# The down product of the routed slots, from one fp32 product to three fp32r passes

## What is computed

```python
logits = x @ router_w.T
top_vals, top_idx = jax.lax.top_k(logits, 1)          # one of 8 experts for each token
scores = sigmoid(logits where chosen, -inf elsewhere)
gate, up = split((x * score) @ gate_up_proj[e])        # 256 -> 2 x 512
routed = (up * silu(gate)) @ down_proj[e]              # 512 -> 256
shared = silu(x @ shared_gate_w) * (x @ shared_up_w) @ shared_down_w
out = layernorm(x + shared + routed)
```

## Time and profile before

| | us |
|---|---|
| median of 3 runs | 579.01 (578.83 to 580.04) |
| the profiled execution | 578.61 |
| its span in the profile | 576.8 |
| PE busy | 558.0 (97%) |
| DVE busy | 391.8 (68%) |
| POOL busy | 302.8 (52%) |
| ACT busy | 225.6 (39%) |

### The profile page before, as it was taken

How to read it: one execution, slowest core, us unless ns; L and a number is a source line. 1 busy time by engine, 2 the same in 40 slices (tenths; PEclk the granted TensorE clock), 3 DMA queues, 4 the chain that set the end, 5 groups by cost and what they waited for, 6 DMA issues and landing times.

```text
span 576.8 us, 11184 instructions
## 1 busy us (share of the span) xinstructions
PE 558.0 (97%) x3732; PEld 458.9 (80%) x3732; DVE 391.8 (68%) x826; ACT 225.6 (39%) x403; POOL 302.8 (52%) x311
## 2 busy tenths in 40 slices
PE   7998989999999999999999899999999999999994
PEld 5776778788788788788787687888888888888883
DVE  5888987878877877877876786555644544445543
ACT  3434532553552552552542674133333333333331
POOL 0544592492492492492482555347675555555544
PEclk9999999999999999999999999999999999999998
DMA  7901207203203204501281503822343222222211
GB/s 259 299 6 38 74 2 52 97 1 75 74 1 75 74 2 74 183 2 38 76 362 40 219 19 98 269 57 67 72 84 85 83 74 82 68 80 82 75 47 36
DMA packets 37430, 50.48 MB, mean 88 GB/s; under 512 B 10576, under 2 KB 29520, under 8 KB 37360
## 3 DMA queue, kind: packets, MB, share of 16 engines
q1 hardware_dynamic: 28128, 31.24, 19.0%
q0 software_dynamic: 6048, 15.39, 9.5%
q10 hardware_dynamic: 3200, 3.15, 1.6%
HBM read 36.21 MB, written 13.96 MB: 87 GB/s over the span
## 4 chain that ended last, share of the span: by engine, by line
PE 84%; DVE 5%; issue 4%; POOL 3%; ACT 1%; DMA 0%; POOLq 0%; DVEq 0%; ACTq 0%
PE duo L1484 47%; PE duo L1856 11%; PE duo L1706 6%; PE duo L1540 5%; PE duo L1562 4%; PE duo L1866 3%; PE duo L1696 1%; PE duo L1750 1%; PE duo L1710 1%; PE duo L1644 1%; POOL turned L819 1%; PE duo L1686 1%; PE duo L1602 1%; PE duo L1620 1%; DVE sims L1009 1%
## 5 line engine op out<-in xcount | busy, mean ns | idle before, releaser
L1484 PE MATMUL duo<-w_gu_hi,xsT 128*128 x312 | 107.0, 404 | 0.0
L1484 PE MATMUL duo<-x1T,wsgu 128*128 128x512 f32 x384 | 93.1, 395 | 0.0
L1484 PEld LDWEIGHTS duo<-x1T,wsgu 128*128 128x128 f32 x384 | 70.9, 188 | 15.3
L1433 DVE SCALAR_TENSOR_TENSOR eh<-duo,seat,e_act 128x512 f32<-128x512 f32 x39 | 29.3, 751 | 76.9 <-PE duo L1484 72.0
L1856 PE MATMUL duo<-w_dn,ehT 128*128 x312 | 73.9, 380 | 0.8 <-ACT ehT L802 0.8
L819 POOL TENSOR_TENSOR turned<-turned,swapped 128x1024 f32<-128x1024 f32 x16 | 38.5, 2425 | 67.2 <-DVE swapped L1000 67.2
L938 POOL DMA_INDIRECT out_rows<-of,seat x39 | 39.7, 1018 | 55.8 <-DVE of L1452 52.8
L1484 PEld LDWEIGHTS duo<-w_gu_hi,xsT 128*128 128x128 f32 x312 | 58.6, 188 | 11.3
L1856 PEld LDWEIGHTS duo<-w_dn,ehT 128*128 128x128 f32 x312 | 56.3, 190 | 7.1 <-issue 1.0
L1484 PE MATMUL duo<-w_gu,xsT 128*128 x156 | 60.6, 389 | 0.0
L1009 DVE TENSOR_TENSOR sims<-duo,causal 128x512 f32<-128x512 f32 x64 | 41.2, 686 | 15.9 <-ACT sims L594 15.9
(11 more groups left out here) (171 smaller groups left out, 1131.8 us busy)
## 6 DMA issues: line engine op xcount, KB each, us to landing
w_gu<-L_ffn_gate_up_proj SPq DMA_DIRECT2D x8, 1024.0 KB, 8.3
x_in<-x_t SPq DMA_DIRECT2D x8, 512.0 KB, 6.4
x_res<-L_attn_x SPq DMA_DIRECT2D x8, 512.0 KB, 4.0
xz_d<-zs SPq DMA_DIRECT2D x8, 512.0 KB
xz_d<-x SPq DMA_DIRECT2D x7, 512.0 KB, 4.9
w_dn<-L_ffn_down_proj SPq DMA_DIRECT2D x4, 512.0 KB, 6.2
w_dn<-L_ffn_down_proj ACTq DMA_DIRECT2D x4, 512.0 KB, 8.2
rot<-rotation SPq DMA_DIRECT2D x4, 256.0 KB, 6.9
```

Of the source, the lines that this page charges most:

```text
L1433: nc.vector.scalar_tensor_tensor(out=eh[:, :], in0=duo[s % 2][:, 1, :], scalar=f32(seat[:, s, :])[:, 2:3], in1=e_act[:, :], op0=ALU.mult, ...
L1484: last = mm(out_, left(a, k), right(b, k), start=start and k == 0 and n == 0, stop=stop and k == kt - 1 and n == len(PASSES) - 1)
```

## The change

The down product of the slots is made in three fp32r passes. The high halves of the down weights (`w_dn`, now fp32r) stay on chip for all experts. The low halves don't fit there beside them. In steps 2 to 6 (one expert in steps 2 and 3, two in 4 to 6) the raw weights of one expert are loaded (SP), rounded to `dn_top` (ACT), subtracted to `dn_low` (POOL), and both halves written to DRAM (SP). `w_dn` is then filled from the high halves in DRAM, for experts 5 to 7 at the end of step 7 where it was in step 6. In the slots SP loads the low half of the slot's expert, 512 KB, into a ring of three. The low half of `ehT` is made by DVE from PSUM. `ehT_lo` lies over `wo`, the ring `dn_rest` over `x1T` and `x1`, and `dn_raw`, `dn_top`, `dn_low` where w_dn of experts 5 to 7 comes to lie.

```diff
+RESTS = 3
+PARTED = {2: (0,), 3: (1,), 4: (2, 3), 5: (4, 5), 6: (6, 7)}
...
+        dn_hi_d = scratch("dn_hi_d", [EXPERTS * P, FT * D])
+        dn_lo_d = scratch("dn_lo_d", [EXPERTS * P, FT * D])
...
+        dn_rest = sb("dn_rest", [P, RESTS, FT * D], F32R)
...
# SP, in step(t)
+                if t - 1 in PARTED:
+                    down_parts_out(PARTED[t - 1][-1])
+                if t in PARTED:
+                    down_raw_in(PARTED[t][0])
                 if has(t - 2):
                     sp.wait_ge(sig.x1_ok, TILES * (t - 1))
...
-                if t == PAIRS - 2:
-                    down_in(5)
-                    down_in(6)
-                    down_in(7)
...
+                if t in PARTED and len(PARTED[t]) > 1:
+                    down_parts_out(PARTED[t][0])
+                    down_raw_in(PARTED[t][1])
                 if has(t - 2) and t < PAIRS:
                     sums_out(t - 2)
+                if t == PAIRS - 1:
+
+                    sp.wait_ge(sig.dn_top_out, 16 * EXPERTS)
+                    sp.wait_ge(sig.dn_low_out, 16 * EXPERTS)
+                    down_in(5)
+                    down_in(6)
+                    down_in(7)
...
+            def down_raw_in(e):
+
+                sp.wait_ge(sig.dn_low_ok, e)
+                sp.dma_start(dn_raw[:, :].rearrange("p (k n) -> p k n", k=FT), down[e].rearrange("(k p) n -> p k n", p=P))\
+                    .then_inc(sig.dn_raw_in, 16)
+
+            def down_parts_out(e):
+                rows = slice(P * e, P * (e + 1))
+                sp.wait_ge(sig.dn_low_ok, e + 1)
+                sp.dma_start(dn_hi_d[rows, :], f32(dn_top[:, :])).then_inc(sig.dn_top_out, 16)
+                sp.dma_start(dn_lo_d[rows, :], f32(dn_low[:, :])).then_inc(sig.dn_low_out, 16)
...
+            def rest_in(s):
+
+                if s >= RESTS:
+                    sp.wait_ge(sig.ed_ps, s - RESTS + 1)
+                e = sp.value_load(slot_ei[0:1, one(s)], min_val=0, max_val=EXPERTS - 1)
+                sp.dma_start(f32(dn_rest[:, (s + 2) % RESTS, :]), dn_lo_d[bass.ds(e * P, P), :])\
+                    .then_inc(sig.rest_in[s % RESTS], 16)
...
# SP, before and in the slots
-            for s in range(5):
+            for s in range(3):
                 seat_load(s)
 
+            sp.wait_ge(sig.zs_ok, 2 * (PAIRS - 1))
+            sp.wait_ge(sig.x1_out, 16 * PAIRS)
+            rest_in(0)
+            for s in range(3, 5):
+                seat_load(s)
+
+            sp.wait_ge(sig.gu_ps, 2 * FT * PAIRS)
+            rest_in(1)
             sums_out(PAIRS - 1)
+            rest_in(2)
...
+            for s in range(RESTS, SLOTS):
+                rest_in(s)
+                if ahead < EARLY:
+                    for _ in range(3):
...
# ACT
+            def down_top(e):
+
+                act.wait_ge(sig.dn_raw_in, 16 * (e + 1))
+                if e:
+                    act.wait_ge(sig.dn_top_out, 16 * e)
+                    act.wait_ge(sig.dn_low_ok, e)
+                nc.scalar.activation(dn_top[:, :], dn_raw[:, :], ACT.Copy).then_inc(sig.dn_top_ok, 1)
...
                     shared_act(f, 0)
                     h_high(f, 0)
+                    if t in PARTED:
+                        down_top(PARTED[t][0])
                     shared_act(f, 1)
...
                     if t == 3:
                         expert_hi(EXPERTS - 2)
+                    if t in PARTED and len(PARTED[t]) > 1:
+                        down_top(PARTED[t][1])
...
             for e in range(4):
-                act.dma_start(w_dn[:, e, :, :], down[e].rearrange("(k p) n -> p k n", p=P)).then_inc(sig.edn_in, 16)
+                act.dma_start(f32(w_dn[:, e, :, :]).rearrange("p f d -> p (f d)"), dn_hi_d[P * e:P * (e + 1), :])\
+                    .then_inc(sig.edn_in, 16)
...
# POOL
+            def down_rest(e):
+
+                pool.wait_ge(sig.dn_top_ok, e + 1)
+                if e:
+                    pool.wait_ge(sig.dn_low_out, 16 * e)
+                nc.gpsimd.tensor_tensor(dn_low[:, :], dn_raw[:, :], f32(dn_top[:, :]), ALU.subtract)\
+                    .then_inc(sig.dn_low_ok, 1)
...
                     residual(a)
+                if t in PARTED:
+                    down_rest(PARTED[t][0])
                 if has(f) and t <= PAIRS:
                     take_seats(f)
+                if t in PARTED and len(PARTED[t]) > 1:
+                    down_rest(PARTED[t][1])
...
# DVE
+            def hidden_lo(s):
+
+                dve.wait_ge(sig.ehT_ok, s + 1)
+                if s:
+                    dve.wait_ge(sig.ed_ps, s)
+                nc.vector.tensor_tensor(ehT_lo[:, :, :], duo[2][:, 0, :].rearrange("p (f n) -> p f n", f=FT),
+                                        f32(ehT[:, :, :]), ALU.subtract).then_inc(sig.ehT_low_ok, 1)
...
                     slot_sum(s - 1)
+                if is_slot(s):
+                    hidden_lo(s)
...
# PE
             def slot_down(s, e):
-                pe.wait_ge(sig.ehT_ok, s + 1)
+                pe.wait_ge(sig.ehT_low_ok, s + 1)
+                pe.wait_ge(sig.rest_in[s % RESTS], 16 * (s // RESTS + 1))
...
                 for f in range(FT):
-                    last = mm(duo[2][:, 1, 0:D], ehT[:, f, :], dn_flat[:, bass.ds(e * (FT * D) + f * D, D)],
-                              start=(f == 0), stop=(f == FT - 1))
+                    weights = (dn_flat[:, bass.ds(e * (FT * D) + f * D, D)],
+                               dn_rest[:, (s + 2) % RESTS, f * D:(f + 1) * D])
+                    for n, (left, right) in enumerate(PASSES):
+                        last = mm(duo[2][:, 1, 0:D], halves[left][:, f, :], weights[right],
+                                  start=f + n == 0, stop=f == FT - 1 and n == len(PASSES) - 1)
```

More of the change, by code:

```diff
@@ L172, in build @@
         sb = tensors(ctx)
[L173 removed]
+        w_dn = sb("w_dn", [P, EXPERTS, FT, D], F32R)
         w_gu = sb("w_gu", [P, EXPERTS, KT, 2 * FF])
@@ L192, in build @@
         eh = sb("eh", [P, FF])
-        ehT = sb("ehT", [P, FT, P])
+        ehT = sb("ehT", [P, FT, P], F32R)
         of = sb("of", [P, OUTS, D])
@@ L357, in build @@
             edn_in = new("edn_in")
+            dn_raw_in = new("dn_raw_in")
+            dn_top_ok = new("dn_top_ok")
+            dn_low_ok = new("dn_low_ok")
+            dn_top_out = new("dn_top_out")
+            dn_low_out = new("dn_low_out")
+            rest_in = [new(f"rest_in{i}") for i in range(RESTS)]
+            ehT_low_ok = new("ehT_low_ok")
             ew_hi = new("ew_hi")
@@ L540, in _ @@
             sp.wait_ge(sig.scat, 16 * (NTILE - TILES))
-            for s in range(5):
+            for s in range(3):
                 seat_load(s)
+            sp.wait_ge(sig.zs_ok, 2 * (PAIRS - 1))
[5 more added lines that the diff above has]
+            rest_in(1)
             sums_out(PAIRS - 1)
-            for s in range(5, EARLY):
+            rest_in(2)
+            for s in range(5, 11):
                 seat_load(s)
-            sp.wait_ge(sig.plan_ok, 4)
-            sp.wait_ge(sig.scat, 16 * NTILE)
-            for s in range(EARLY, SLOTS):
-                seat_load(s)
+            ahead = 11
+            for s in range(RESTS, SLOTS):
+                rest_in(s)
+                if ahead < EARLY:
+                    for _ in range(3):
+                        if ahead < EARLY:
+                            seat_load(ahead)
+                            ahead += 1
+                elif s >= 13 and ahead < SLOTS:
+                    if ahead == EARLY:
+                        sp.wait_ge(sig.plan_ok, 4)
+                        sp.wait_ge(sig.scat, 16 * NTILE)
+                    for _ in range(2):
+                        if ahead < SLOTS:
+                            seat_load(ahead)
+                            ahead += 1
             sp.wait_ge(sig.out_done, 16 * SLOTS)
@@ L1835, in _ @@
                        w_gu[:, :, :, :].rearrange("p e k n -> p (e k n)").bitcast(F32R))
+            halves = (ehT, ehT_lo)
             dn_flat = w_dn[:, :, :, :].rearrange("p e f n -> p (e f n)")
```

20 lines of the change are left out of this document (13 added, 7 removed).

## The result

The changed kernel takes **572.21 us**, median of 4 runs (570.0 to 572.99), beside 578.92 of the kernel before on the same chip (4 runs, 578.58 to 580.04). The ratio is 0.9873, 95% interval 0.985 to 0.9896. The forecast was 570.3 us, 567.8 to 575.0: the sign is right, the median lies in the stated range, and 1.9 us of the gain did not come. The profiled execution took 572.99 us, the slowest of the four, 2.1 of it around its span.

A forecast was written before the change was run, and what follows sets the result against it. PE was taken as the bound, busy throughout slots and attention steps. Terms -10.6 + 0.65 + 0.9 + 0.4 = -8.65 took the profiled 578.61 to 569.96, stated as 570.3 us; range 567.8 to 575.0, own range 567.8 to 572.

The forecast's parts named there:

- The slots' down product: PE in the slots: twelve fp32r passes at 0.1215 us replace 1.73 us, saving 0.272 per slot, 10.6 us over 39.
- Rival C: Slots' down product: PE's sequencer sets the pace or register-addressed passes are no faster; 579 to 581 us, chance 0.05.
- Rival D: Nothing is blocked and passes take 0.120 us: 567.9 us, lower end of the forecast's range, sharing its 0.70 chance.
- "Cost 0" for the new DVE step in the slots: `hidden_lo`, 0.68 us per slot, fits DVE's idle time with 1.4 us left, so it costs nothing.
- the 0.3 feared for `eh` in four slots: Routing plan behind `hidden_lo` on DVE in slots 2, 4, 6, 7: at most 0.3 us each if cover were gone.
- The sentence on bandwidth: Slots: 73 GB/s now, 108 more from the fetch; gathers on the same DMA engines are issued slots ahead of use.
- rival B: Low half lands late in the slots, PE waits at `rest_in`; at 15 us delay 594 us, chance 0.06.
- The fetch itself: SP's 512 KB load per slot lands within 9.3 of the 13.1 us available, so it costs nothing.
- Step 2: POOL's `down_rest` subtraction blocks DVE's small `spot` and `hT_lo`, lengthening PE's wait at `shared_down`: +0.9 us.
- Steps 3 to 6: Making low halves: +0.4 us (0 to 0.9) in step 3, where a shift has no slack; 0 in steps 4 to 6.
- rival A: Steps pay more: ACT waits for second raw loads in steps 4 to 6, DVE against POOL; 572 to 575.7 us, chance 0.19.
- The tail: Last slot: nothing covers `hidden_lo` and its handover before the down product, +0.65 us.

The follow-up runs named there:

- e1: Changed kernel with no low-half fetch from slot 3 on, stale ring contents used instead: 569.36 us, ratio 0.9837.
- e4: Changed kernel with DVE's `slot_norm` placed behind `slot_sum` and `hidden_lo` in each slot: 572.27 us, ratio 0.9878.
- e8: e3 with `slot_norm` behind `slot_sum` and `hidden_lo`, the old order kept in the last rounds: 568.45 us, ratio 0.9827.
- e9: e8 with DVE's second `hT_lo` in step 2 made between the two halves of the group norm: 566.45 us, ratio 0.979.
- e11: The changed kernel, unchanged, run again in the session of the other experiments: 570.7 us, ratio 0.9862.
- e10: The kernel before with only the second `hT_lo` in step 2 moved between the group norm's halves: 576.58 us, ratio 0.9962.
- e2: Changed kernel with the low halves of steps 2 and 3 both made in step 3: 568.94 us, ratio 0.9841.
- e3: Changed kernel with POOL's low-half subtraction in step 2 moved behind the seat scatters: 568.78 us, ratio 0.9827.
- e5: e3 fetching only 64 of 128 partitions of each low half from slot 3 on: 570.02 us, ratio 0.9844.
- e6: e3 with the whole low half fetched in rows of 1 KB instead of 4 KB: 569.76 us, ratio 0.9839.
- e7: The kernel before with one extra DVE addition ahead of the `hT_lo` PE waits for in step 2: 579.94 us, ratio 1.0016.

## Why the prediction was right, and where it was wrong

**The slots' down product** (-10.6): right, and a little small. The period fell by 0.295 instead of 0.272, since the passes go at 0.120 us; that is 11.2 for the 38 intervals between 39 slots, where the forecast's figure is 10.3, and the slots of e1, e4, e8 and e9 show 11.0 to 11.3 (195.65 against 184.36 to 184.63). Rival C is refuted by the same rows; the small matmuls at 0.059 were the right evidence against it. Rival D's pace came, but not its clear path.

**"Cost 0" for the new DVE step in the slots**: this step failed. It held `hidden_lo` against DVE's own load, 1.4 us left, and that was right: the 0.3 feared for `eh` in four slots did not come. What it did not ask is what stands ahead of `hidden_lo` on DVE and waits for another engine. `slot_norm` does, for POOL, which waits for a landing, and the change adds the traffic that makes the landing late. It cost 2.7 us in the profiled execution and 0.5 in others. The sentence on bandwidth looked at the fetch and the gathers only; the scatters were named in rival B, but as a load on the fetch. For the gathers it counted on their being issued early enough; single ones were late for PE after all, by 0.2 to 0.5 us.

**The fetch itself**: right. It landed in 4.4 us, where 12.0 were left after its issue (13.1 - 1.1), so rival B is refuted. Its suspicion of the shared DMA engines was sound, only the transfer that suffered was the other one.

**Step 2** (+0.9): the block between POOL and DVE was right. The small operation was blocked too, by 0.57 us, as taken. PE's wait grew by this 0.57, not by 0.9: the subtraction ended at 84.24, which is 83.98 in the times of the trace before, 0.2 sooner than taken, and `spot` ended with it, where the 0.9 had let it begin there. By the Trainium skill (SBUF — State Buffer, Who interferes with whom) the lock holds for the whole instruction; the trace agrees, `spot` takes 0.76 us instead of 0.19, ending with POOL's 2.81. What was missing is the clock: in most runs of the changed kernel, and in e11, it costs another 1.5 us, more than twice the 0.57. The price of a PE wait was taken as its length.

**Steps 3 to 6** (+0.4): nothing at all. The outputs of steps 2 to 7 follow each other at 43.1 us, as before. ACT did wait for the second raw load in each of steps 4 to 6 (1.06, 1.09 and 2.58 us), the place that rival A named, but its copy in step 4 ended at 178.84, 4.1 us ahead of its next work, and PE has no wait from it. Rival A is refuted, though its time range fits the result: 572 came from two other places.

**The tail** (+0.65): right. +0.35 was measured from the last hidden transposes to the end, and this stretch holds the last of the 39 shorter down products, so the forecast's own figure for it is 0.65 - 0.27 = +0.38. The step from the hidden transposes to the last down product grew by 0.72 (2.10 against 1.38), where 0.75 was forecast.

The sum by what was measured in the profiled execution: -11.3 in the slots as e1 shows them undisturbed, +2.7 of slot waits, +0.57 and +1.5 in step 2, +0.35 at the end, +0.26 start-up, is -5.9. The forecast's own terms measure -11.3 + 0.57 + 0 + 0.35 = -10.4, where it had -8.65; e8, in which the two unforeseen costs are all but absent (0.2 us in the slots, a fallen clock in one run of five), stands at 568.45 against 578.69, -10.2. The two, the slots' waits and the clock, are 4.2 in this execution. That the median missed the forecast by 1.9 only is in part luck: the forecast's own terms came out 1.7 us better than it had them, against the 4.2. And 572.21 lies just above the forecast's own range, which ended at 572; the stated range holds it because it was widened to 575.0 for rival A, which did not happen.

**What stays open**: what decides whether the clock falls behind a given wait, and why the scatters' lateness reaches PE by 0.5 us in one execution and 2.7 in another, and whether the last pair's seat scatters on POOL have a part in it.

## What to carry to other kernels

When a new step is put into an engine's queue, its cover isn't the idle time of that engine alone: look at what stands ahead of it and waits for someone else, and follow that wait to its end, to a DMA's landing if it goes there. A large prefetch that is itself never late can still hurt, through the small transfers whose completions somebody waits for one by one. And a wait of some 2 us on a TensorE that is otherwise always busy should be priced at more than its length, and closing it by a change of order (here worth 2.2 us to the kernel before, e10) comes before any arithmetic.

## What the runs showed of the hardware that was not expected

- The granted clock of a TensorE that is busy all the time can fall to the lower level after a single wait, and each fall costs about 1.3 to 1.5 us. By groups of runs: no wait, 0 of 10 (e9, e10); 1.8 us, 12 of 54 (the kernel before as it ran beside the experiments, e2, e3, e5, e6, e8); 2.4 us, 16 of 24 (the changed kernel's first four runs, e1, e4, e7). The four runs of e11 (2.36 us) are not in these counts, since they form no clear groups; its profiled run had the fall. Which runs had it is judged by their time and mean clock, which agree but for one run (579.88 us at 0.998); the profiled executions show it directly, in step 2 of the changed kernel, e4, e5, e6 and e11, and nowhere else before PE's last matmuls.
- Scatters of 128 rows of 1 KB, each waited for before the next, left POOL waiting for a landing 4.2 us in all (376 to 566 us) at 80 GB/s of traffic, 23.7 at 132 and 33.6 to 42.4 at 180 to 187, while the DMA share was only 0.62. The same traffic with the scatters handed over later in the slot gave 9.8 to 11.1 (e4, e8, e9), so such a sum measures the order of work as well as the landings.
- 12 fp32r passes of 256 columns, with weights at addresses from a register, run at 0.120 us each, with 46 ns of sequencer work per three passes hidden; so does the fp32 form before, with 46 ns per product.
- A DVE product of 128x32 is blocked by POOL's 128x1024 subtraction to its end, as a large one is. The subtraction itself takes 2.81 us there, where the shortest of the eight in the same trace takes 2.38. The small product is hardly the reason: in the trace the long `hT_lo` (79.75 to 82.02) still runs for the subtraction's first 0.6 us, and in the kernel before POOL's 128x8 copy behind the same `hT_lo` takes 0.65 us instead of 0.18.
